# Two chained attention layers on one core: the low part of k made by VectorE, and group 14 shifted on VectorE in place of group 12

## What is computed

```
# layer 0, per image (64 inner channels)
g = g_w x + g_b;  theta = theta_w x + theta_b;  phi = phi_w x + phi_b
y = softmax(theta^T phi) g                 # 4096 x 4096 scores
mid = W_w y^T + W_b + x
# layer 1, per image (128 channels, scale 128**-0.5)
q = Wq mid + bq;  k = Wk mid + bk;  v = Wv mid + bv
out = mid + (softmax(scale * q^T k) v)^T
```

## Time and profile before

| | |
|---|---|
| median of 3 runs | 3179.99 us (3179.93 to 3180.76) |
| the profiled execution | 3179.93 us |
| its span in the trace | 3178.1 us |
| granted TensorE clock, mean | 0.998 of full |
| busy share of the span: PE, PEld, DVE, ACT, POOL | 99%, 65%, 71%, 58%, 92% |

### The profile page before, as it was taken

The page is one execution under the profiler, slowest core; times in us unless marked ns, Lnnn a source line. Parts: engine busy times, 40 slices in busy tenths (PEclk is TensorE's granted clock), DMA queues, the critical chain, the costliest instruction groups (busy, mean ns, idle before and its releaser), DMA issues. The chain is left out here.

```text
span 3178.1 us, 42122 instructions
## 1 busy us (share of the span) xinstructions
PE 3138.3 (99%) x15488; PEld 2054.2 (65%) x15488; DVE 2249.7 (71%) x2724; ACT 1832.2 (58%) x2378; POOL 2914.8 (92%) x1546
## 2 busy tenths in 40 slices
PE   8999999999999999999999999999999999999997
PEld 4555545557777755555777775554577777777775
DVE  6666777767777767776777776777677777777773
ACT  4555555546666555554666655555566666666665
POOL 5999999988999989998999999999899999999997
PEclk9999999999999999999999999999999999999999
DMA  1000000006657540001666654000175766657575
GB/s 57 27 24 24 27 28 27 25 25 136 137 118 146 111 103 25 27 28 31 137 128 130 142 111 95 27 27 27 34 144 115 146 133 128 131 116 146 113 141 118
DMA packets 91934, 271.41 MB, mean 85 GB/s; under 512 B 10192, under 2 KB 10320, under 8 KB 91728
## 3 DMA queue, kind: packets, MB, share of 16 engines
q0 software_dynamic: 55296, 201.35, 32.8%
q1 hardware_dynamic: 36432, 67.36, 7.0%
HBM read 50.57 MB, written 16.78 MB: 21 GB/s over the span
## 5 line engine op out<-in xcount | busy, mean ns | idle before, releaser
L1214 POOL TENSOR_TENSOR p_lo<-probs,p_hi 128x1024 fp32r<-128x1024 f32 x448 | 1162.6, 2639 | 110.2 <-ACT probs L947 82.4
L410 POOL TENSOR_TENSOR sums<-sums,probs 128x1024 f32<-128x1024 f32 x448 | 1067.0, 2382 | 84.7 <-ACT probs L959 18.4
L1081 DVE TENSOR_TENSOR probs<-scores,shift_rows 128x1024 f32<-128x1024 f32 x512 | 626.2, 1223 | 369.7 <-PE scores L619 362.0
L1057 DVE TENSOR_REDUCE piece_max<-rough 128x2 f32<-128x1024 f32 x504 | 615.0, 1220 | 303.8 <-PE rough L567 302.8
L946 ACT ACTIVATE p_hi<-probs 128x1024 fp32r<-128x1024 f32 x448 | 475.0, 1060 | 568.2 <-DVE probs L1081 568.0
L1051 DVE TENSOR_REDUCE piece_max<-rough 128x1 f32<-128x512 f32 x1024 | 661.3, 682 | 125.8 <-PE rough L561 125.8
L947 ACT ACTIVATE probs<-probs 128x1024 f32<-128x1024 f32 x512 | 535.5, 1046 | 89.2 <-DVE probs L1081 89.2
L959 ACT ACTIVATE probs<-scores 128x1024 f32<-128x1024 f32 x377 | 382.4, 1023 | 338.0 <-PE scores L606 329.4
L615 PE MATMUL scores<-qry_a,keys_a 128*128 128x512 f32 x1024 | 441.9, 432 | 0.0
L1248 POOL DMA_DIRECT2D sent_sums<-probs x384 | 413.1, 1076 | 0.0
L619 PE MATMUL scores<-qry_b,keys_a 128*128 128x512 f32 x1024 | 400.1, 391 | 0.0
(11 more groups left out here) (104 smaller groups left out, 4204.1 us busy)
## 6 DMA issues: line engine op xcount, KB each, us to landing
sent_sums<-probs POOLq DMA_DIRECT2D x384, 512.0 KB, 4.9
x_res<-x SPq DMA_DIRECT2D x32, 256.0 KB, 2.9
mid<-mid_new SPq DMA_DIRECT2D x32, 256.0 KB, 2.4
x_kv<-mid SPq DMA_DIRECT2D x32, 256.0 KB, 2.8
x_q<-mid SPq DMA_DIRECT2D x32, 256.0 KB, 2.8
x_res<-mid SPq DMA_DIRECT2D x32, 256.0 KB, 4.5
out<-result SPq DMA_DIRECT2D x32, 256.0 KB, 3.6
x_q<-x SPq DMA_DIRECT2D x31, 256.0 KB, 2.8
```

Of the source, the lines that this page charges most:

```text
L410: eng.tensor_tensor(sums[:], sums[:], probs[:, slot(st, s)], ALU.add).then_inc(s_plus, 1)
L1057: nc.vector.reduce_max(piece_max[:, t, TPG * c:TPG * (c + 1)], src, AX.X).then_inc(s_reduced, 1)
L1081: nc.vector.tensor_tensor(probs[:, slot(st, s)].rearrange("p (h c) -> p h c", c=QB), scores[:, s % 2].rearrange("p (h c) -> p h c", c=QB), ...
L1214: nc.gpsimd.tensor_tensor(dst, w, rd(hi), ALU.subtract).then_inc(done, 1)
```

## The change

In the three kv stages `split_k` moves from GpSimd to VectorE, at the same step 12 (24 instructions of 128 x 512, both inputs in SBUF). In stage 6 it stays on GpSimd. In `MOVED` group 14 takes the place of group 12, so that in 27 blocks group 12 gets the fourth product and a direct exponential, and group 14 is shifted by VectorE. ScalarE's exponential of group 14 is put into step 15, behind the copy of the shift row and of the query, ahead of the one of group 15.

```
-MOVED = (0, 1, 2, 12, 15)
+MOVED = (0, 1, 2, 14, 15)
...
-                    if s in st.moved and s < GROUPS - 1:
+                    if s in st.moved and s < GROUPS - 2:
                         probs_moved(st, s)
...
                     if s in st.moved and s == GROUPS - 1:
+                        probs_moved(st, s - 1)
                         probs_moved(st, s)
...
+            def split_k(n, keys, c):
+
+                dve.wait_ge(h_k, n + 1)
+                nc.vector.tensor_tensor(cols(keys_b[keys], c), whole[:], rd(cols(keys_a[keys], c)),
+                                        ALU.subtract).then_inc(l_k, 1)
...
                     reduce(behind_values, s)
+                    if s == K_LO_AT and st.layer == 0 and st.stage.prepares == "kv":
+                        split_k(st.stage.made * BLOCKS + st.i, st.stage.made_keys, st.i)
...
-                    if s == K_LO_AT and stage.prepares in ("kv", "late"):
+                    if s == K_LO_AT and st.layer == 1 and stage.prepares == "late":
                         split_k(stage.made * BLOCKS + st.i, stage.made_keys, st.i)
```

## The result

| | before | after |
|---|---|---|
| median of 6 runs, us | 3180.01 (3179.66 to 3180.76) | 3192.89 (3192.64 to 3193.66) |
| span of the profiled execution, us | 3178.1 | 3191.2 |
| ratio, with its 95% interval | | 1.0041 (1.003 to 1.0051) |

A forecast was written before the change was run, and what follows sets the result against it. The prediction took the block's tail (pair 16, its reduction, shift row, value matmul) as the bound, not nearly full GpSimd. Gains of 2.9 in kv blocks and 3.1 in stage 0, 6.0 us, gave 3174.0 us; range 3170.5 to 3196.

The forecast's parts named there:

- part 2: split_k moved to VectorE in the kv stages: worth nothing by itself, its cost on VectorE taken as 0.
- the 0: Cost of split_k on VectorE, taken as none because VectorE's shifts hold 1.21 us beside running adds.
- The upper bound of 1.5 us a block: Highest price of split_k on VectorE: a full GpSimd add, 2.38 us, less the 0.9 of cover.
- Rival A: kv blocks: split_k waits for GpSimd's running add, both reading SBUF; 1.4 us a block, 3194 us; chance 0.35.
- just too late: Rival A: VectorE asks for split_k at 34.16, group 11's add starts at 34.0; wait 2.2 us.
- the case without it: The forecast, with no collision or VectorE first: 3174.0 us, chance 0.45.
- If VectorE always asks first: Under Rival A: split_k holds up the add by 0.6 us, GpSimd's cycle is 39.9, below the block; forecast stands.
- Part 1: Group 14 moved for group 12: 16 kv blocks gain 2.9 us, stage 0's blocks 0 to 6 gain 3.1.
- Block 1 of those stages: kv stages' block 1 has no v_lo and starts with 0.54 already: nothing gained.
- The late exponentials: Exponentials 14 and 15 in a row on ScalarE: 0.1 us a block if tight, taken as nothing.
- rival C: Late exponentials and shifts of groups 14, 15 take back at the block's head the tail's gain: 3178 to 3181; chance 0.08.
- GpSimd's relief: GpSimd loses 24 split_k, cycle 40.32 to 39.2 us: worth nothing itself, keeps it below a 40.1 to 40.2 block.

The follow-up runs named there:

- experiment 3: Changed kernel with split_k replaced by a VectorE maximum reading only `whole`, low part of k left out in layer 0's kv stages: 3174.03 us, ratio 0.9981.
- experiment 7: Changed kernel plus a GpSimd subtraction of 128 x 128 in a spare tile at step 2 of each kv block: 3183.23 us, ratio 1.0013.
- Experiment 8: Changed kernel plus a GpSimd subtraction of 128 x 256 in a spare tile at step 2 of each kv block: 3175.2 us, ratio 0.9984.
- experiment 1: Changed kernel with split_k back on GpSimd, group 14 still in place of group 12: 3174.05 us, ratio 0.9982.
- experiment 5: Changed kernel with split_k one step earlier on VectorE, ahead of a reduction it waits 2 us for: 3173.68 us, ratio 0.9982.
- experiment 6: Changed kernel with split_k as two VectorE instructions of 128 x 256: 3259.8 us, ratio 1.0249.

## Why the prediction was wrong

- **The step that failed** is in part 2: "I take the 0 because VectorE's shifts, one input in PSUM and one in SBUF, hold 1.21 us beside running adds." The shifts have one input from SBUF; split_k has two, and experiment 3 shows that this is the difference that counts. The earlier trace rows could not carry that step, and the earlier trace rows had its one instruction with two such inputs from a time when GpSimd was done. With no row for the case, the 0 was a choice between two ends, and it was put down as if a neighbouring row had settled it. The upper bound of 1.5 us a block was sound: the 14 steady blocks that collided paid 1.26 each against part 1 alone ((14.3 + 3.4) / 14), the three blocks 1 another 1.5 between them (1.2 of it in stage 1), 19 us in all.
- **Rival A** had the right working, row by row. It put the add of group 11 at 34.0 to 36.4 behind the value matmul and VectorE's request at 34.16. Read on the same scale (0.41 us behind the shift row, 519.62) the add ran from 33.99 to 36.38, and VectorE asked at 34.17. It waited 2.1 us (2.77 - 0.68) where 2.2 were given, and some 0.8 of it was covered where 0.9 were. Its own kv blocks came to 41.50, as "41.5" says. It counted 16 or 17 blocks at the full price; 15 waited in full and four in part, since VectorE was first in block 0 of stage 1 and in block 5 of stage 3. Its sum does not follow from its terms, though, and that its 3194 lies 1 us from the measured time is in part luck: 2.2 less 0.9 is 1.3 a block and not 1.4, and 3174.0 and its own 23 us are 3197; the 20 that it adds stands nowhere in its working. It is near the 19 us that the runs give.
- **The weight** was the second mistake. The rival's condition was a margin of 0.16 us, "just too late", and experiment 7 shows that 0.05 us is enough to lose. The time was worked out to that accuracy, and nothing in the profile spoke against the mechanism, yet the case without it had the greater chance.
- **A margin in the other direction** was foreseen too: "If VectorE always asks first ... the forecast stands." Experiment 8 is that case but for block 1 of stages 3 and 5: 3175.2, the add 0.3 longer where 0.6 was foreseen, the steady blocks unchanged (40.27 for 40.25 in the mean).
- **Part 1** was right. Stage 0: 3.1 us foreseen, 3.3 measured, and its blocks at 40.5 with no wait of the g projection for `keys_a` left. The 16 kv blocks: 2.9 foreseen, 3.4 + 0.4 = 3.7 measured, 0.23 each for 0.18. Block 1 of those stages: "nothing" foreseen, 0.7 lost in the three. That fits the 0.23 us by which pairs 15 and 16 come later, a step the prediction names itself and then left out for the blocks that have no v_lo to win it back from. The two misses cancel. Block 7 of stage 0 lost 0.1, as said.
- **The late exponentials** of groups 14 and 15 cost nothing that experiment 1 shows; rival C is out. Its blocks at 40.24 are what the forecast had, 40.1 to 40.25.
- **GpSimd's relief is worth nothing**: right, by experiment 5 against experiment 1. The prediction also said that it keeps GpSimd below a block of 40.1 to 40.2. That wasn't needed: in experiment 1, with the low part of k on GpSimd, the block still came down to 40.24. GpSimd fell behind it by 0.02 to 0.34 us a block, and block 7, where it has idle time, took that up.

## What to carry to other kernels

Before an elementwise instruction goes to VectorE, count its inputs from SBUF: with two, and a GpSimd that reads SBUF all the time, its price is its own length plus up to one whole GpSimd instruction, so it belongs where VectorE has idle time behind it that covers the wait (experiment 5), in as few instructions as possible (experiment 6). Whether it pays that price can hang on less than 0.2 us of phase, so a place where it happens to go well is no good place either: any edit on another engine can move it. And where a forecast has to choose between two bounds without a row that shows the case, the choice is the risk, and its chance should be no better than the evidence for it.

## What the runs showed of the hardware

- The exclusion shows as a longer instruction and never as idle time: split_k 0.68 us when it is first, and 2.70 to 2.92 in the steady blocks where it is behind an add; the add 2.39 alone, 2.76 when VectorE was 0.15 us ahead and 2.89 when it was 0.03 ahead. Waits for semaphores stand ahead of an instruction in the timeline, this one stands in it. The view of waits shows only its second victim, TensorE, and blames the reduction.
- It holds for a whole instruction and passes on in between: a half of 128 x 256 (0.41 us alone) waited as long as the whole did.
- VectorE asking 0.05 us behind GpSimd waits 2.2 us; asking 0.03 us ahead it waits none. The tie is narrow: in experiment 7 it lost once by 0.02 us and won once with a recorded start 0.01 us behind that of the add.
- A column of constants in SBUF doesn't count as an input. The prediction says that inside the stages each VectorE instruction takes at most one input from SBUF, which holds only if the columns are left out. `qry_b`, below, reads `qry_a` and such a column (`const_sb`) from SBUF; all 64 of the kernel before last 0.749 to 0.755 us, and 59 of them lie wholly inside an elementwise instruction of GpSimd, this one in an add that runs from 601.54 on.

```profile
602.77 0.75 DVE L1062 SCALAR_TENSOR_TENSOR qry_b<-rough,const_sb,qry_a 128x512 fp32r<-128x512 f32 x1 [0.84 <-ACT qry_a L880]
```

- On GpSimd an elementwise instruction of 128 x 128 lasted 0.4 us and pushed the next by 0.17; one of 128 x 256 lasted 0.61; a fill of 128 x 128 lasted 0.20 and pushed the next by nothing.
- TensorE's clock had no part in the 13 us: it was 0.998 of full in both kernels. (The one slice below full of the profile before is the last of the 40, at 0.92, and not the first, which is at 1.00.) In experiment 6 it had a part: 3.40 us of idle time were followed by a stretch at 0.56, 1.17 us in the changed kernel by one at 1.00.
